# A staging loop in a hybrid attention and mixture-of-experts kernel: four slots in place of two, and its store moved to another queue

## The chip, the cores and the metric

One Trainium2 chip, one launch on its 8 cores. Every core runs the same program on one batch row of 2048 tokens of 1024 numbers, with no exchange between cores. The metric is the device time of the slowest core in microseconds (us).

## The reference

Per batch row (S = 2048 tokens, D = 1024, 16 heads) the layer is a random-feature attention, an FFN block, a channel attention, and the same FFN block again. Only the latent attention `mla` inside the FFN block matters here:

```python
def _L0_ffn_ref(x, ...):
    x = x + mla(rmsnorm(x, w_ln1), W_kvd, W_qd, W_ku, W_qu, W_vu, W_ropeq, W_ropek, W_o)
    x = x + moe(rmsnorm(x, w_ln2), Wg_s, Wu_s, Wd_s, Wg_r, Wu_r, Wd_r, W_router, routing_bias)
    return x

def mla(xn, ...):
    ...
    scores = jnp.where(causal[None, None], scores, jnp.finfo(scores.dtype).min)
    probs = jax.nn.softmax(scores, axis=-1)
    y = jnp.einsum('bhqk,bkhd->bqhd', probs, v).reshape(B, S, H)
    return y @ W_o

x = x + _L0_attn_a_ref(_layernorm(x), ...)
x = x + _L0_ffn_ref(_layernorm(x), ...)
x = x + _L0_attn_b_ref(_layernorm(x), ...)
x = x + _L0_ffn_ref(_layernorm(x), ...)
```

## The kernel before

The kernel is written against the five instruction queues by hand. `Prog` (lines 36 to 94) keeps a list for each engine; each instruction of it is preceded by its semaphore waits, so an engine runs its list strictly in order, and a wait holds up everything behind it on that engine. `p.dma(eng, ...)` puts a DMA in the list of `sync` (SP) or `gpsimd` (POOL); its completion adds 16 to the semaphore given. `p.release(name, sem)` notes when a buffer comes free and `p.use(name)` gives the wait for that. Vector instructions add 1 to `s_dv`, matmuls add 1 to `s_mm`.

`phase_mla` (from line 707) runs twice in the program, once in each FFN block. Its flash loop goes over two halves of 8 heads, 4 blocks of 512 queries (`qb`) and the key blocks below the diagonal. The unnormalized output of a head, 64 rows by 512 queries, and one row of softmax sums leave PSUM through a VectorE cast into `SCF[:, 1536:2048]` (buffer `stg`) and are stored by POOL into `d_yraw`, a DRAM tensor of 1040 rows (1024 of values, 16 of sums) by 2048 tokens, with semaphore `s_yd`. `v_yq[qb]` is the count at which query block `qb` is complete for all heads.

Behind the flash loop stands the loop that the change is about (lines 1071 to 1090), once for each of 16 tiles of 128 tokens, `l` = 0 to 15. Call its steps:

- T, on SP: a DMA transpose of `d_yraw[:, 128 l : 128 l + 128]` into a slot of `SCB`, so that tokens lie on partitions. It waits for `v_yq[l // 4]`, the end of the V projection (`vmm_latdone`), and the slot.
- the scaling, on VectorE: a reciprocal of the 16 sums into `STAT[:, 112:128]`, a drain, and 16 multiplications of 64 columns each in place.
- W, on SP: a plain DMA of the slot to `d_y2` (token-major, DRAM), which waits for the last multiplication.

There are two slots (`ytk0`, `ytk1`), each released by W's landing. As T and W are both in SP's list, the order there is T0, W0, T1, W1, and so on: T of the next tile stands behind W of this one, and so behind this tile's scaling.

Then SP transposes `d_y2` back into `SCA`, 8 DMAs for each half of the tokens (lines 1095 to 1110); every one waits for the one ahead of it. The first of them waits also for `(s_dv, s_dv.v)`, that is for VectorE's last multiplication of tile 15. The matmuls with `W_o` (lines 1111 to 1126) of tokens 0 to 1023 wait for the first 8. In the profile the program's `d_y2` is shown as `d_y`.

The queue of POOL holds, around this, the stores of `d_yraw` before the loop, and behind it the weight loads of the mixture of experts, the first of which waits until the `W_o` matmuls are done.

```python
w = [(s_yd, v_yq[l // 4]), (s_mm, vmm_latdone)]
w = list(w) + p.use(f"ytk{l % 2}")
vt = p.dma("sync", slot, APx(d_yraw, 128 * l, [[S, 1040], [1, 128]]),
           s_tp, wait=w, transpose=True)
```

Of the kernel before, what the change touches and what calls it, by code (L numbers as in the profile page):

```python
# [12 lines left out]
S, D, NT, ND = 2048, 1024, 16, 8  # L13
# [86 lines left out]
def APx(t, off, dims):  # L100
    return bass.AP(t, off, [list(d) for d in dims])


def build_nc(stop_after=None):
# [44 lines left out]
    d_y2 = nc.dram_tensor("d_y2", [S, D], BF16, kind="Internal")  # L149
# [4 lines left out]
    def sbt(name, shape, dt=F32):  # L154
        g = nc.sbuf_tensor(name, list(shape), dt)
        t = g.__enter__()
        ctx.append(g)
        return t
# [13 lines left out]
    SCB = sbt("SCB", [128, 8192], BF16)  # L172
# [22 lines left out]
    p = Prog(nc)  # L195
    s_ld = p.sem("s_ld")
    s_tp = p.sem("s_tp")
    s_st = p.sem("s_st")
    s_gld = p.sem("s_gld")
    s_mm = p.sem("s_mm")  # L200
    s_dv = p.sem("s_dv")
    s_ac = p.sem("s_ac")
    s_pp = [p.sem(f"s_pp{i}") for i in range(4)]
    s_wl = [p.sem(f"s_wl{i}") for i in range(3)]
    s_dbg = p.sem("s_dbg")
    s_rl = [p.sem(f"s_rl{i}") for i in range(4)]
    s_tb = p.sem("s_tb")
    s_sc = p.sem("s_sc")
    s_yd = p.sem("s_yd")

    def mm(out_ap, lhsT, rhs, start, stop, wait=(), tp=None):
        def b(e, out_ap=out_ap, lhsT=lhsT, rhs=rhs, start=start, stop=stop, tp=tp):
            return e.matmul(out_ap, lhsT, rhs, start=start, stop=stop, tile_position=tp)  # L213
        return p.on("tensor", b, wait=wait, inc=s_mm, n=1)

    def v_op(name, *a, wait=(), **kw):
        def b(e, name=name, a=a, kw=kw):
            return getattr(e, name)(*a, **kw)  # L218
        return p.on("vector", b, wait=wait, inc=s_dv, n=1)
# [52 lines left out]
    for c in range(ND):  # L272
        v_op("tensor_scalar_mul", STAT[:, ER * c:ER * c + ER],
             STAT[:, ER * c:ER * c + ER], WLN2[:, c:c + 1],
             wait=([(s_ld, v_preload), (s_ld, v_wrt)] if c == 0 else ()))
# [434 lines left out]
    def phase_mla(v_xnt, v_gain):  # L710
        vmm0 = s_mm.v

        def vcol(l):
# [9 lines left out]
              wait=p.use("wb0"))  # L723
# [5 lines left out]
        for (wb, woff, swl, wv_, dsto) in ((WB1, 4096, s_wl[1], vl_wb1, 0),  # L729
                                           (WB1, 6144, s_wl[1], vl_wb1, 4096)):  # L730
            for ic in range(2):
                for lb in range(4):
# [3 lines left out]
                    for c in range(ND):  # L736
# [5 lines left out]
                           wait=(w0 if c == 0 else ()))  # L742
# [11 lines left out]
        for h2 in range(2):  # L754
            for c2 in range(2):
                hc = 2 * h2 + c2
                kro = 8320 + 4096 * h2 + 2048 * c2
                for lb in range(4):
# [4 lines left out]
                    for c in range(ND):  # L763
# [4 lines left out]
                           wait=(w0 if c == 0 else ()))  # L768
# [15 lines left out]
        vmm_latdone = 0  # L784
        for h2 in range(2):
            v_scpre = s_sc.v
            for pr in range(4):
                gp = 4 * h2 + pr
                for lb in range(4):
# [3 lines left out]
                    for ic in range(2):  # L793
# [4 lines left out]
                           wait=(w0 if ic == 0 else ()))  # L798
# [4 lines left out]
                         wait=[(s_mm, vm)] + ([(s_sc, v_scpre)]  # L803
                                              if pr == 0 and lb == 0 else []))
# [41 lines left out]
            for pr in range(4):  # L846
                gp = 4 * h2 + pr
                for lb in range(4):
# [3 lines left out]
                    for ic in range(2):  # L852
# [6 lines left out]
                           wait=(w0 if ic == 0 else ()))  # L859
# [46 lines left out]
            if h2 == 1:  # L906
                p.release("wb2", s_mm)
                vmm_latdone = s_mm.v
# [8 lines left out]
            for hl in range(8):  # L917
# [3 lines left out]
                if par == 0:  # L921
                    for pj in range(2):
# [7 lines left out]
                              s_sc, wait=w0)  # L930
# [10 lines left out]
                    for kb in range(4):  # L941
# [3 lines left out]
                           wait=p.use(f"ps{bk}") + [(s_dv, v_sqk)])  # L945
# [8 lines left out]
                    for kb in range(4):  # L954
                        p.release(f"ps{kbank[kb]}", s_dv)
                    v_op("tensor_mul", SCF[:, 0:2048], qslab, qslab,
                         wait=[(s_mm, vmm_k)])
                    p.drain("vector")
                    v_sqq = s_dv.v
                    for qb in range(4):  # L960
# [3 lines left out]
                           wait=p.use(f"ps{bk}") + [(s_dv, v_sqq)])  # L964
# [11 lines left out]
                    for qb in range(4):  # L976
# [9 lines left out]
                         wait=[(s_mm, vm_mh)] + p.use("mhcols"))  # L986
# [7 lines left out]
                for qb in range(4):  # L994
# [4 lines left out]
                    for kc in range(nkc):  # L999
# [8 lines left out]
                        if prev is not None:  # L1008
# [5 lines left out]
                               wait=[v_pt, (s_dv, v_vh)] + (w5 if pkc == 0 else []))  # L1014
# [9 lines left out]
                        else:  # L1024
                            if jst > 0:
# [3 lines left out]
                                 wait=[(s_mm, vm), (s_dv, v_mh)] + (wpt if jst == 0 else []))  # L1029
# [3 lines left out]
                                 wait=[(s_ac, va)])  # L1033
# [9 lines left out]
                       wait=[v_pt, (s_dv, v_vh)] + (w5 if pkc == 0 else []))  # L1043
                    p.release(f"pt{pslot}", s_mm)
                    if qb == 3:
# [5 lines left out]
                         wait=[(s_mm, vm_pv)] + wst)  # L1051
                    p.drain("vector")
                    p.release("ps5", s_dv)
                    vd = s_dv.v
# [14 lines left out]

        v_y2h1 = None  # L1070
        for l in range(NT):
            slot = SCB[:, (l % 2) * 1040:(l % 2) * 1040 + 1040]
            w = [(s_yd, v_yq[l // 4]), (s_mm, vmm_latdone)]
            w = list(w) + p.use(f"ytk{l % 2}")
            vt = p.dma("sync", slot, APx(d_yraw, 128 * l, [[S, 1040], [1, 128]]),
                       s_tp, wait=w, transpose=True)
            v_op("reciprocal", STAT[:, 112:128], slot[:, 1024:1040],
                 wait=[(s_tp, vt)])
            p.drain("vector")
            for h_ in range(H):  # L1080
                v_op("tensor_scalar_mul", slot[:, 64 * h_:64 * h_ + 64],
                     slot[:, 64 * h_:64 * h_ + 64], STAT[:, 112 + h_:113 + h_])
            p.drain("vector")
            vd = s_dv.v
            p.dma("sync", APx(d_y2, 128 * l * D, [[D, 128], [1, D]]), slot[:, 0:1024],
                  s_pp[l % 2], wait=[(s_dv, vd)])
            p.release(f"ytk{l % 2}", s_pp[l % 2])
            if l == 7:
                v_y2h1 = (s_pp[0].v, s_pp[1].v)
        v_y2 = (s_pp[0].v, s_pp[1].v)  # L1090
        if stop_after == "mla_trip":
            dump_dbg()
            return True
# [2 lines left out]
        for half in range(2):  # L1096
            for c in range(ND):
                src = APx(d_y2, half * 1024 * D + c * 128, [[D, 1024], [1, 128]])
                w = [(s_tp, s_tp.v)]
                if c == 0 and half == 0:  # L1100
                    w += [(s_pp[0], v_y2h1[0]), (s_pp[1], v_y2h1[1]),
                          (s_mm, vmm_latdone), (s_dv, s_dv.v)]
                elif c == 0:
                    w += [(s_pp[0], v_y2[0]), (s_pp[1], v_y2[1])]
                p.dma("sync",
                      SCA[:, c * S + 1024 * half:c * S + 1024 * half + 1024],
                      src, s_tp, wait=w, transpose=True)
            if half == 0:
                v_y2t_h1 = s_tp.v
# [199 lines left out]
    def phase_ffn(call):  # L1309
# [7 lines left out]
        if phase_mla(v_xnt, v_gain):  # L1317
            return True
# [284 lines left out]
```

How the kernel before makes its waits and increments, by code:

```python
        def f(e, build=build, w=w, inc=inc, n=n):  # L54
            for s, v in w:
                e.wait_ge(s.h, v)
            ins = build(e)
            if inc is not None:
                ins.then_inc(inc.h, n)
# [6 lines left out]
        def f(e, ps=ps):  # L66
            for s, v in ps:
                if v > 0:
                    e.wait_ge(s.h, v)
```

## Time and profile before

| | us |
|---|---|
| median of the 2 runs shown | 7717.26 (7558.05 and 7876.47) |
| profiled execution, device time | 7573.67 |
| its span, slowest core (core 2) | 7571.9 |
| spans of all 8 cores | 7530.7 to 7571.9 |
| busy in that span: TensorE / VectorE / ScalarE / GpSimd | 5157.2 / 2487.9 / 1403.9 / 243.4 |

The span of a core runs from its first instruction to its last. Busy times of engines overlap, and a share of the whole span is a mean over stages with different limits, so the stretch of the loop has to be read by itself. In the rows, PE is TensorE's matmuls, PEld its weight loads, DVE is VectorE, ACT ScalarE, POOL GpSimd, SP SyncE; a "q" behind the name (SPq, DVEq) is the engine's instruction queue. L213, L218, L223, L78 and L79 are the helpers through which matmuls, VectorE and ScalarE operations, DMA transposes and plain DMAs are issued, so instructions are told apart by their tiles. `A<-B` writes A from B. PEclk is the granted TensorE clock as a share of its full 2.4 GHz.

### The profile page before, as it was taken

The page shows a single profiled execution, that of the slowest core. Times are in us where ns is not written, and L with a number is a line of the kernel's source. Part 1 is how long each engine was busy: PE and PEld are TensorE (multiplying, and loading weights), DVE is VectorE, ACT ScalarE, POOL GpSimd, SP SyncE. Part 2 cuts the span into 40 slices and gives each one's busy share as a digit, 9 for nine tenths or more (in the row PEclk, how much of TensorE's full clock was granted, in tenths as well). Part 3 has the DMA queues.
Part 4 walks back from the last instruction along what each step waited for, and adds up shares of the span by engine and source line. Part 5 has one row for each costly group of instructions (what it writes and reads, how often), then busy time and mean ns, then how long its engine had stood idle before and what let it go on. Part 6 is the DMA issues. An engine that isn't in the chain of part 4 may idle for free.

```text
span 7571.9 us, 83246 instructions; the slowest of 8 cores (7530.7 to 7571.9 us)
## 1 busy us (share of the span) xinstructions
PE 5157.2 (68%) x21469; PEld 2065.1 (27%) x21856; DVE 2487.9 (33%) x5348; ACT 1403.9 (19%) x2392; POOL 243.4 (3%) x403
## 2 busy tenths in 40 slices
PE   3556554565662587999996864565652677999995
PEld 1222222111110233444442422111110333444442
DVE  3333335324222413222223455324222423222221
ACT  1221220242441101111111010342441101111110
POOL 0000000000000000000000000000000000000000
PEclk9556566677665798999997976677675788999997
DMA  3001112001002431222224021001002431222223
GB/s 80 4 6 17 17 34 61 9 12 19 13 10 57 102 67 21 36 34 45 34 34 76 3 42 50 10 11 23 10 9 62 96 67 23 34 45 34 34 34 89
DMA packets 280243, 277.60 MB, mean 37 GB/s; under 512 B 181649, under 2 KB 188177, under 8 KB 279826
## 3 DMA queue, kind: packets, MB, share of 16 engines
q0 software_dynamic: 81776, 154.36, 12.3%
q1 hardware_dynamic: 198050, 117.89, 6.1%
q8 instruction: 236, 3.87, 0.2%
q14 instruction: 181, 1.48, 0.1%
HBM read 287.73 MB, written 63.05 MB: 46 GB/s over the span
## 4 chain that ended last, share of the span: by engine, by line
PE 59%; DVE 12%; issue 9%; ACT 8%; DMA 6%; DVEq 2%; SPq 1%; ACTq 1%; another core or an unknown queue 0%; POOL 0%; POOLq 0%
PE PS L213 59%; ACT SCF L223 6%; DVE SCF L218 3%; DVE XNT L218 2%; DVE SCB L218 2%; DVEq L73 2%; DVE SM L218 2%; ACT SCA L223 1%; DMA SCB<-d_yraw 1%; DVE SCA L218 1%; DVE STAT L218 1%; SPq L78 1%; DMA d_lo<-SCB 1%; DMA sp_x<-R 1%; DMA SCA<-d_y 1%
## 5 line engine op out<-in xcount | busy, mean ns | idle before, releaser
L213 PE MATMUL PS<-XNT,WB 128*128 128x512 bf16 x9272 | 2068.6, 383 | 97.1 <-ACT SCA L223 52.7
L213 PE MATMUL PS<-WB,SCA 128*128 128x512 bf16 x4766 | 1091.9, 389 | 357.4 <-DMA SCA<-d_y 267.5
L213 PEld LDWEIGHTS PS<-XNT,WB 128*128 128x128 bf16 x9472 | 933.5, 99 | 1225.6 <-issue 142.3
L223 ACT ACTIVATE SCF<-PS,SM 128x512 bf16<-128x512 f32 (+3 forms) x1280 | 771.2, 622 | 1100.2 <-PE PS L213 1008.2
L213 PE MATMUL PS<-SCF,SCA 128*128 128x512 bf16 x1238 | 595.5, 481 | 400.0 <-DVE SCF L218 195.7
L223 ACT ACTIVATE SCA<-PS 128x512 bf16<-128x512 f32 x768 | 444.7, 595 | 2242.0 <-PE PS L213 1998.9
L218 DVE TENSOR_TENSOR SCA<-SCA,PS 128x512 bf16<-128x512 bf16 x512 | 352.5, 688 | 1438.8 <-PE PS L213 1332.3
L213 PEld LDWEIGHTS PS<-WB,SCA 128*128 128x128 bf16 x4864 | 481.5, 100 | 958.9 <-issue 442.5
L213 PE MATMUL PS<-XNT,SCA 128*128 128x512 bf16 x1270 | 619.5, 501 | 44.5 <-ACT SCF L223 18.9
L218 DVE SCALAR_TENSOR_TENSOR R<-PS,STAT,R 128x512 f32<-128x512 f32 x448 | 315.7, 747 | 515.9 <-PE PS L213 515.9
L213 PE MATMUL PS<-IDENTB,SCF 128*128 128x128 bf16 x768 | 97.2, 305 | 509.3 <-DVE SCF L218 509.3
L218 DVE TENSOR_TENSOR SCF<-SCF,CONSTB 128x128 bf16<-128x128 bf16 x512 | 106.3, 208 | 980.0 <-ACT SCF L223 975.9
L213 PEld LDWEIGHTS PS<-SCF,SCA 128*128 128x128 bf16 x1280 | 128.1, 100 | 884.5 <-issue 861.8
L223 ACT ACT_TABLE_LOAD x16 | 20.5, 1283 | 1430.7 <-PE PS L213 696.4
L213 PE MATMUL PS<-WB,XNT 128*128 128x512 bf16 x997 | 232.3, 385 | 7.5 <-DVE SCA L218 4.5
L218 DVE TENSOR_TENSOR R<-PS,R 128x512 f32<-128x512 f32 x192 | 129.8, 690 | 317.6 <-PE PS L213 317.6
L223 ACT ACTIVATE SCF<-R 128x1024 bf16<-128x1024 f32 x96 | 101.4, 1057 | 636.7 <-PE PS L213 442.3
L213 PEld LDWEIGHTS PS<-IDENTB,SCF 128*128 128x128 bf16 x768 | 73.6, 132 | 533.6 <-issue 533.0
L213 PEld LDWEIGHTS PS<-XNT,SCA 128*128 128x128 bf16 x1280 | 128.1, 100 | 324.9 <-issue 324.9
L213 PE MATMUL PS<-SCB,WB 128*128 128x512 bf16 x252 | 91.9, 485 | 183.0 <-DVE XNT L218 181.9
L79 POOL DMA_DIRECT2D d_yraw<-SCF x256 | 132.3, 521 | 2282.1 <-DVE SCF L218 2247.3
L213 PE MATMUL PS<-SCF,CONSTB 128*128 128x512 bf16 (+1 forms) x158 | 61.2, 522 | 198.6 <-DVE SCF L218 198.6
(121 smaller groups left out, 2667.7 us busy)
## 6 DMA issues: line engine op xcount, KB each, us to landing
WB<-wg_r POOLq DMA_DIRECT2D x28, 1024.0 KB, 13.7
WB<-wu_r POOLq DMA_DIRECT2D x28, 1024.0 KB, 24.0
WB<-wd_r POOLq DMA_DIRECT2D x28, 1024.0 KB, 13.0
sp_x<-R SPq DMA_DIRECT2D x8, 2048.0 KB, 16.7
R<-sp_x POOLq DMA_DIRECT2D x8, 2048.0 KB, 28.3
R<-x SPq DMA_DIRECT2D x4, 2048.0 KB
SCA<-XNT SPq DMA_DIRECT2D x32, 256.0 KB, 2.9
d_yraw<-SCF POOLq DMA_DIRECT2D x128, 64.0 KB, 1.9
```

What stands on the lines that cost most here:

```text
L73: self.q[eng].append(lambda e: e.drain())
L78: return e.dma_start(out=out, in_=in_, transpose=True)
L79: return e.dma_start(out=out, in_=in_)
L213: return e.matmul(out_ap, lhsT, rhs, start=start, stop=stop, tile_position=tp)
L218: return getattr(e, name)(*a, **kw)
L223: return getattr(e, name)(*a, **kw)
```

## The change

The loop gets four slots in place of two (`ytk0` to `ytk3`, 4 x 1040 columns of `SCB`). T signals one of four semaphores `s_pp[l % 4]` in place of the shared `s_tp`. W moves from the `sync` list to the `gpsimd` list and signals `s_rl[l % 4]`, which now releases the slot. The waits of the transposes behind the loop name the four new semaphores in place of two. VectorE's instructions are the same. A semaphore `s_y2` is added and never used.

```diff
         for l in range(NT):
-            slot = SCB[:, (l % 2) * 1040:(l % 2) * 1040 + 1040]
+            slot = SCB[:, (l % 4) * 1040:(l % 4) * 1040 + 1040]
             w = [(s_yd, v_yq[l // 4]), (s_mm, vmm_latdone)]
-            w = list(w) + p.use(f"ytk{l % 2}")
+            w = list(w) + p.use(f"ytk{l % 4}")
             vt = p.dma("sync", slot, APx(d_yraw, 128 * l, [[S, 1040], [1, 128]]),
-                       s_tp, wait=w, transpose=True)
+                       s_pp[l % 4], wait=w, transpose=True)
             v_op("reciprocal", STAT[:, 112:128], slot[:, 1024:1040],
-                 wait=[(s_tp, vt)])
+                 wait=[(s_pp[l % 4], vt)])
             p.drain("vector")
             for h_ in range(H):
                 v_op("tensor_scalar_mul", slot[:, 64 * h_:64 * h_ + 64],
                      slot[:, 64 * h_:64 * h_ + 64], STAT[:, 112 + h_:113 + h_])
             p.drain("vector")
             vd = s_dv.v
-            p.dma("sync", APx(d_y2, 128 * l * D, [[D, 128], [1, D]]), slot[:, 0:1024],
-                  s_pp[l % 2], wait=[(s_dv, vd)])
-            p.release(f"ytk{l % 2}", s_pp[l % 2])
+            p.dma("gpsimd", APx(d_y2, 128 * l * D, [[D, 128], [1, D]]),
+                  slot[:, 0:1024], s_rl[l % 4], wait=[(s_dv, vd)])
+            p.release(f"ytk{l % 4}", s_rl[l % 4])
             if l == 7:
-                v_y2h1 = (s_pp[0].v, s_pp[1].v)
-        v_y2 = (s_pp[0].v, s_pp[1].v)
+                v_y2h1 = [(s_rl[i], s_rl[i].v) for i in range(4)]
+        v_y2 = [(s_rl[i], s_rl[i].v) for i in range(4)]
...
                 if c == 0 and half == 0:
-                    w += [(s_pp[0], v_y2h1[0]), (s_pp[1], v_y2h1[1]),
-                          (s_mm, vmm_latdone), (s_dv, s_dv.v)]
+                    w += v_y2h1 + [(s_mm, vmm_latdone), (s_dv, s_dv.v)]
                 elif c == 0:
-                    w += [(s_pp[0], v_y2[0]), (s_pp[1], v_y2[1])]
+                    w += v_y2
```

## Rows read from the trace of the kernel before

**Rows 1.** Waits of core 2: who waited for whom, total us, times, longest.
```profile
PE PS L213 <- DMA SCA<-d_y: 267.5, 2, 135.1
DVE STAT L218 <- DMA SCB<-d_yraw: 120.4, 30, 4.5
```

**Rows 2.** Busy time by stretch; columns as the first line names them.
```profile
core 2: us, PE busy (x) PEld busy (x) DVE busy (x) ACT busy (x) POOL busy (x), PEclk, DMA share, GB/s
2331.70:2435.60 103.90, 0.00 (x0) 0.00 (x0) 43.03 (x272) 0.00 (x0) 1.02 (x2) 0.50 0.30 77
2463.10:2475.60 12.50, 12.47 (x44) 5.15 (x46) 3.46 (x5) 2.30 (x4) 0.00 (x0) 0.76 0.43 75
2475.70:2486.40 10.70, 10.68 (x49) 4.90 (x50) 4.15 (x6) 3.45 (x6) 0.00 (x0) 1.00 0.43 75
```

**Rows 3.** Chain of work that ended last, first block: start us, us, what.
```profile
2331.73 0.25 DVE STAT L218
2332.08 0.82 DVE SCB L218 x5
2333.05 1.47 DVE SCB L218 x10
2334.60 0.35 SPq L79
2335.11 2.99 DMA SCB<-d_yraw
2338.19 0.25 DVE STAT L218
...
2432.76 0.25 DVE STAT L218
...
2435.61 0.34 SPq L79
2436.25 3.30 DMA SCA<-d_y
```

**Rows 4.** The same chain in the second block, its first and last step.
```profile
5723.66 0.25 DVE STAT L218
...
5830.11 3.42 DMA SCA<-d_y
```

**Rows 5.** SP's instructions in order of time: start us, us, instruction.
```profile
2295.73 1.20 SPq L78 DMA_TRANSPOSE SCB<-d_yraw  x1
2334.60 0.35 SPq L79 DMA_DIRECT2D d_y<-SCB  x1
```

**Rows 6.** VectorE and POOL in order of time; in brackets idle time and releaser.
```profile
2314.68 0.69 DVE L218 CAST SCF<-PS 65x512 bf16<-65x512 f32 x1 [0.80 <-PE PS L213]
2315.94 1.04 POOL L79 DMA_DIRECT2D d_yraw<-SCF  x2 [11.87 <-DVE SCF L218]
2330.89 0.69 DVE L218 CAST SCF<-PS 65x512 bf16<-65x512 f32 x1 [0.80 <-PE PS L213]
2332.08 2.43 DVE L218 TENSOR_SCALAR SCB<-SCB,STAT 128x64 bf16<-128x64 bf16 x16
2333.79 1.02 POOL L79 DMA_DIRECT2D d_yraw<-SCF  x2 [16.80 <-DVE SCB L218]
2338.54 2.43 DVE L218 TENSOR_SCALAR SCB<-SCB,STAT 128x64 bf16<-128x64 bf16 x16
```

**Rows 7.** DMA issues: count, KB each, median us from issue to landing.
```profile
d_yraw<-SCF POOLq DMA_DIRECT2D x128, 64.0 KB, 1.9
d_y<-SCB SPq DMA_DIRECT2D x32, 256.0 KB, 2.1
SCB<-d_yraw SPq DMA_TRANSPOSE x32, 3.3
SCA<-d_ya SPq DMA_TRANSPOSE x8, 5.4
```

**Rows 8.** Transposes of 2048 rows back to back on SP, and who waited.
```profile
1017.03 21.66 SPq L78 DMA_TRANSPOSE SCA<-d_ya  x8
1041.33 3.19 PE L213 MATMUL PS<-WB,SCA 128*128 128x512 bf16 x7 [29.12 <-DMA SCA<-d_ya]
```

**Rows 9.** One SP transpose while weights load through POOL's queue.
```profile
6178.06 13.02 SPq L78 DMA_TRANSPOSE SCB<-d_xn  x1
```

More of the change, by code:

```diff
@@ L209, in build_nc @@
     s_yd = p.sem("s_yd")
+    s_y2 = p.sem("s_y2")
     def mm(out_ap, lhsT, rhs, start, stop, wait=(), tp=None):
```

## The prediction

> **What bounds the kernel now.** I read first the waits, for what TensorE, the busiest engine, waits on longest. It stands still twice, 267.5 us together and up to 135.1 us at a time, until the transposes of `d_y` into `SCA` land [rows 1]. These are the ends of the two `phase_mla` calls. The table by stretch shows what goes on in the first: in the 103.9 us of the loop TensorE and ScalarE do nothing, VectorE is busy for 43.03 us, the 16 DMA engines for 0.30 of the time [rows 2]. So nothing is full there; it is latency. The chain of waits then shows one tile as a ring of single steps [rows 3]: scaling from 2331.73 to 2334.52 (2333.05 + 1.47), W's issue at 2334.60, T's issue at 2335.11, its landing 2.99 later, the next scaling at 2338.19. From 2331.73 to the last reciprocal at 2432.76 it is 15 periods of (2432.76 - 2331.73) / 15 = 6.74 us. Of one period 2.79 us is VectorE, and the other 3.9 us are SP's two issues and T's landing. VectorE's wait for T says the same: 120.4 us in 30 times [rows 1]. From the first reciprocal to the first transpose behind the loop it is 2436.25 - 2331.73 = 104.5 us in the first block, and 5830.11 - 5723.66 = 106.5 us in the second [rows 3, 4].
>
> **What the change does to it.** It removes from SP's list, between T of one tile and T of the next, W and with it the wait for the scaling.
>
> *The first four T.* T0 is issued at 2295.73, long before the flash loop ends [rows 5], since it needs only query block 0. T1 to T3 need the same block and now stand right behind it. At an issue of 1.20 us each and 3.3 us to land [rows 5, 7] they are in place by about 2295.7 + 4 x 1.2 + 3.3 = 2304, some 28 us before VectorE is free at 2331.7. Their cover is the last head's flash work, and they sit in no list that this uses; cost nothing. If they slowed a store of `d_yraw` the cost would be at most their own 4.8 us of issue.
>
> *VectorE's pace.* With data in place a tile takes 2.79 us, plus the gap to the next reciprocal. The nearest row for the gap is the cast that ends at 2330.89 + 0.69 = 2331.58 ahead of the reciprocal at 2331.73 [rows 3, 6]: 0.15 us. So 2.94 us a tile. All 16 take 15 x 2.94 + 2.79 = 46.9 us. Then SP starts the first transpose of `d_y`: it waits for the last multiplication, as before, but no longer issues W15 first; 0.08 us, as W's issue comes 0.08 behind the scaling today. Loop: 47.0 us.
>
> *W on POOL.* Today W is issued 0.08 us after the last multiplication. POOL is slower to start. A store of `d_yraw` starts 0.57 us after its cast when VectorE then rests (2315.94 against 2314.68 + 0.69), but 2.21 us after it when the multiplications follow at once (2333.79 against 2331.58) [rows 6]; I see the second distance on all eight cores. In the new kernel multiplications always follow, so I take 2.2 us, bounds 0.6 and, if it has to wait for a pause of VectorE, no fixed end (a rival below). The row says nothing of a loss on VectorE: the 16 multiplications with POOL's two issues among them take 2.43 us, as do the 16 without [rows 6]. I take 0; the upper bound is that POOL's issue, 1.02 / 2 = 0.51 us, stops VectorE once in each tile, 15 x 0.51 x 2 = 15 us. Landing of 256 KB: 2.1 us from SP; from POOL 64 KB takes 1.9 [rows 7]. I take 2.3. Behind W in POOL's list stand only other Ws and weight loads that wait for the `W_o` matmuls.
>
> *The slots.* A slot goes round in: T 3.3, scaling 2.79, W's start 2.2, its landing 2.3, and some 0.3 for three wake-ups, together 10.9 us for four tiles, 2.7 us a tile. That is just under VectorE's 2.94. With T at 3.8 and W at 2.9 it is 12.0, 3.0 a tile; over 12 tiles this costs 0.7 us a block. I allow 1 us a block.
>
> *The DMA engines.* Eight transposes of 2048 rows, back to back, take from 1017.03 to TensorE's start at 1041.33, 3.0 us each, though each one needs 5.4 to land [rows 7, 8]. So they overlap, and 1040 rows cost between 1.2 (SP's issue) and 1.5 us. The share of 0.30 of 6.74 us [rows 2] is 2.0 us of work for T and W of a tile, which fits in 2.94.
>
> *What is late next.* The 8 transposes of `d_y` up to the first `W_o` matmul are one after the other in both kernels (each waits for the last), so they stay, some 27 us. W8 to W15 are needed only by the second 8. TensorE's clock: it is granted 0.50, its 1.2 GHz level, through the loop; when matmuls return, 12.5 us at 0.76, then 1.00 (2.4 GHz) [rows 2]. A pause of about 75 us in place of 132 still leaves it at the low level when work returns, so this cost of about 2 us stays as it is. Other phases wait for TensorE or VectorE and shift along.
>
> **The sum.** First block 104.5 - 47.0 = 57.5, second 106.5 - 47.0 = 59.5, together 117.0; less 2 for the slots, 115. The profiled execution took 7573.67: 7573.7 - 115 = 7459 us, 1.5% less. The median shown, 7717.26, is the mean of two runs 318 us apart; the profiled one belongs with the lower (7558.05), and my number is for such a run.
>
> **Rivals.**
>
> *POOL starves.* The long start of 2.21 us could mean that POOL gets in only when VectorE pauses. The page "SBUF — State Buffer" of the Trainium skill, section on the "DVE blocks DMA" trap, has it so: a DMA of GpSimd has its descriptors written through ports that VectorE locks in its fast modes, here `tensor_scalar`. By its strict form no W would start during a run of tiles. VectorE would do the four tiles in the slots, 4 x 2.94 = 11.8 us, then run dry; W starts after about 0.6, lands after 2.3, T lands after 3.3, and with wake-ups there are 6.4 us of idleness. With 16 tiles in fours that is three pauses, 19 us a block, gain 115 - 38 = 77, time 7497 us. For it: the delay. Against it: POOL's issue at 2333.79 falls amid the multiplications, which last to 2334.51 [rows 6]; it got in with no pause. Chance 0.10.
>
> *Only the issue is saved.* The page "DMA: Bandwidth & Descriptors" of the Trainium skill, section "Issuing engines are not separate DMA queues", says that DMAs from several engines share the 16 DMA engines, and that spreading them saves only the time to issue. As a mechanism here: T and W do not overlap, the ring stays, and only W's issue and the step to T (2335.11 - 2334.60 = 0.51 us) go [rows 3]: 32 x 0.51 = 16 us, 7557 us. A milder form, T and W one after the other but beside the scaling, is 3.3 + 2.1 = 5.4 us a tile, gain 15 x 1.34 x 2 = 40, 7534 us. Against both: the overlap of eight transposes and the share of 0.30 [rows 2, 8]. Chance 0.05.
>
> *Slower: T jams beside POOL's queue.* One transpose beside POOL's weight loads held SP for 13.02 us [rows 9]. If each T from T4 on, issued among POOL's stores, took that, the loop would be some 7.5 + 12 x 13.0 + 6 = 170 us, 65 more in each block, and the kernel would take about 7703 us. It decides from about 7.6 us for each T, (104.5 - 13.5) / 12. Against: that one stood behind loads of 1 MB each; here POOL has at most a few 256 KB stores under way. Chance 0.03.
>
> **Chances and range.** Every tile at VectorE's pace, as summed: 0.78, and its own range is 7441 (7558 less 117) to 7474 (7459 plus the 15 us of the bound on VectorE). POOL starves 0.10, only the issue 0.05, slower 0.03, something I have not seen 0.04. The range reaches over the second and third: 7435 to 7560. A measurement of this kernel can tell about 2% from no change. That is 151 us, and VectorE's own work in the two loops, 2 x 47 us out of 211, leaves only 117 to gain. So faster by over 2% has only the unseen and the spread between executions (the two shown differ by more): 0.07. Within 2% 0.90. Slower by over 2% needs more than the jam gives: 0.03.
>
> **What would show it.** In the stretch from the last cast to the first transpose of `d_y`: about 47 us with VectorE over 0.9 busy (43 of 47); reciprocals 2.9 us apart; VectorE's 30 waits for T gone or under 10 us in all; T0 to T3 issued together while the flash loop runs; POOL's stores of `d_y` about 2.2 us behind each last multiplication; the two waits of TensorE for `SCA` down from 267.5 to about 150. POOL starving would show as three gaps of 6 us with Ws in bunches of four. Stretched multiplications (2.9 in place of 2.43 for 16) would show that POOL stops VectorE. I am wrong if the gap between reciprocals is over 3.5 us, or if the gain in the loops is given back behind them.

## The result and the profile after

| | before | changed kernel |
|---|---|---|
| median of all timed executions | 7816.48 us (10) | 7616.62 us (11) |
| executions compared | 7555.31, 7558.05, 7561.08 | 7445.55, 7446.25, 7447.18, 7447.81, 7515.21 |
| profiled execution, not in either row above | 7573.67 us | 7445.2 us |
| mean span of its 8 cores | 7552.6 us | 7435.3 us |

The ratio of the means of the second row is 0.987, 95% interval 0.981 to 0.993: faster, by less than 2%. In the executions left out of that row, of either kernel, the cores of a die show a lower granted clock and take up to 6% longer, which is why the medians of the first row lie 258 and 169 us above those of the second. The medians of the second row are 7558 and 7447 us, 111 us apart (the expectations below start from 7446).

The waits of the slowest core, core 5 (who waited for whom: total us, times, longest), answer to [rows 1]:

```profile
PE PS L214 <- DMA SCA<-d_y: 154.8, 2, 78.1
DVE STAT L219 <- DMA SCB<-d_yraw: 4.3, 6, 1.6
```

TensorE's two pauses fell from 267.5 to 154.8 us. Over the eight cores their mean went from 267.4 to 154.0, 113.4 us less, and the mean span by 117.3: the gain of the loops is the gain of the kernel. VectorE's 30 waits for transposes have become 6.

The pauses hold the loop and the eight transposes of `d_y` behind it. On the mean of the eight cores the loop went from 105.4 to 48.3 us in the first block and from 105.8 to 47.9 in the second, 115.0 less together. The eight transposes behind it take 0.8 us longer in each block (27.9 us where it was 27.1, from the first of them to the first `W_o` matmul), which gives 1.6 back.

The busy time of the same core by stretch, as in [rows 2]:

```profile
core 5: us, PE busy (x) PEld busy (x) DVE busy (x) ACT busy (x) POOL busy (x), PEclk, DMA share, GB/s
2326.10:2375.50 49.40, 0.00 (x0) 0.00 (x0) 42.99 (x272) 0.00 (x0) 9.19 (x17) 0.51 0.58 146
2403.20:2415.70 12.50, 12.47 (x46) 5.11 (x47) 3.46 (x5) 2.30 (x4) 0.00 (x0) 0.78 0.40 77
2415.80:2426.50 10.70, 10.70 (x51) 4.88 (x50) 4.15 (x6) 3.45 (x6) 0.00 (x0) 1.00 0.39 80
```

The same 43 us of VectorE's work now fit in 49.4 us instead of 103.9. TensorE comes back as before: its granted clock is 0.78 over the first 12.5 us (0.76 before), then 1.00.

VectorE in order of time, core 5 (start us, us, instruction, idle time before and its releaser), around the places where it kept its pace and where it lost it:

```profile
2326.16 0.25 DVE L219 RECIPROCAL STAT<-SCB 128x16 f32<-128x16 bf16 x1 [0.16 <-issue]
2326.51 2.43 DVE L219 TENSOR_SCALAR SCB<-SCB,STAT 128x64 bf16<-128x64 bf16 x16
2329.10 0.25 DVE L219 RECIPROCAL STAT<-SCB 128x16 f32<-128x16 bf16 x1 [0.16 <-issue]
...
2347.65 0.25 DVE L219 RECIPROCAL STAT<-SCB 128x16 f32<-128x16 bf16 x1 [0.71 <-DMA SCB<-d_yraw]
2347.99 2.43 DVE L219 TENSOR_SCALAR SCB<-SCB,STAT 128x64 bf16<-128x64 bf16 x16
2351.99 0.25 DVE L219 RECIPROCAL STAT<-SCB 128x16 f32<-128x16 bf16 x1 [1.57 <-DMA SCB<-d_yraw]
...
2373.03 2.43 DVE L219 TENSOR_SCALAR SCB<-SCB,STAT 128x64 bf16<-128x64 bf16 x16
```

The period, from one reciprocal to the next, is 2.94 us (2329.10 - 2326.16). In the first block four of the eight cores keep it nearly throughout and need 47.0 to 47.3 us from the first reciprocal to the first transpose of `d_y`; the others take 47.7 to 51.0 (core 5: 49.4). The chain of waits of core 5 shows what the lost time is made of:

```profile
2341.25 6.12 DMA d_y<-SCB
2347.43 4.47 DMA SCB<-d_yraw
2351.99 0.25 DVE STAT L219
```

One store of a tile took 6.1 us to land and the transpose into its slot 4.5 more, so the round trip of that slot was longer than VectorE's time for four tiles.

POOL, core 5, in order of time. The first row is the last pair of `d_yraw` stores, the second and third are the first two stores of tiles:

```profile
2328.22 1.02 POOL L79 DMA_DIRECT2D d_yraw<-SCF  x2 [16.73 <-DVE SCB L219]
2329.51 0.59 POOL L79 DMA_DIRECT2D d_y<-SCB  x1 [0.27 <-DVE STAT L219]
2332.45 0.55 POOL L79 DMA_DIRECT2D d_y<-SCB  x1 [2.35 <-DVE STAT L219]
```

The multiplications of tile 0 end at 2326.51 + 2.43 = 2328.94 and its store starts 0.57 us later, with the next multiplications already running. The table of DMA issues (median us to landing) gives for the changed kernel:

```profile
d_y<-SCB POOLq DMA_DIRECT2D x32, 256.0 KB, 3.0
SCB<-d_yraw SPq DMA_TRANSPOSE x32, 4.2
```

Both take longer to land than in [rows 7]: 3.0 us where it was 2.1, and 4.2 where it was 3.3.

### The profile page after: what moved, and what is told of

It is laid out like the page before. It is cut to its first block, busy times and chain, and to the rows that moved or that the text cites. A ratio compares the mean times of both kernels' runs of the same rounds, so it can differ in the third digit from the quotient of the medians.

```text
span 7442.8 us, 83639 instructions; the slowest of 8 cores (7426.5 to 7442.8 us)
## 1 busy us (share of the span) xinstructions
PE 5184.5 (70%) x21856; PEld 2061.7 (28%) x21856; DVE 2486.3 (33%) x5348; ACT 1404.7 (19%) x2392; POOL 260.8 (4%) x435
## 4 chain that ended last, share of the span: by engine, by line
PE 61%; DVE 12%; issue 9%; ACT 8%; DMA 5%; DVEq 2%; SPq 1%; ACTq 1%; POOL 0%; POOLq 0%
PE PS L214 61%; ACT SCF L224 7%; DVE SCF L219 3%; DVE XNT L219 2%; DVEq L73 2%; DVE SM L219 2%; DVE SCB L219 2%; ACT SCA L224 1%; DVE SCA L219 1%; DVE STAT L219 1%; SPq L78 1%; DMA SCA<-d_y 1%; DMA sp_x<-R 1%; DMA d_xn<-SCF 1%; DMA d_lo<-SCB 1%
## 5 line engine op out<-in xcount | busy, mean ns | idle before, releaser
L214 PE MATMUL PS<-WB,SCA 128*128 128x512 bf16 x4864 | 1090.0, 387 | 240.9 <-DMA SCA<-d_y 154.8
## 6 DMA issues: line engine op xcount, KB each, us to landing
WB<-wd_r POOLq DMA_DIRECT2D x28, 1024.0 KB, 12.5
```

## The experiments

### Slots alone

Four slots, but the store stays in SP's list. The edit is shown against the changed kernel, as all below.

```diff
-            p.dma("gpsimd", APx(d_y2, 128 * l * D, [[D, 128], [1, D]]),
-                  slot[:, 0:1024], s_rl[l % 4], wait=[(s_dv, vd)])
+            p.dma("sync", APx(d_y2, 128 * l * D, [[D, 128], [1, D]]),
+                  slot[:, 0:1024], s_w4[l % 4], wait=[(s_dv, vd)])
```

> Four slots, with the store of each tile left in SP's list between the transposes. My theory: the ring is made by the order in that list, not by the slots, so the transpose of the next tile still stands behind this tile's scaling; period 6.7 us, first reciprocal to first transpose of d_y about 104.5 and 106.5 us in the two blocks, undisturbed time as before, 7555 to 7575 us. Rival, the slots were what was missing: the period falls to 2.9 us and the time to about 7446 us.

Measured: 7550.5 and 7553.8 us, where the kernel before took 7556, 7559 and 7561 beside it (and once 7613). TensorE's and VectorE's waits on core 1:

```profile
PE PS L215 <- DMA SCA<-d_y: 271.4, 2, 137.3
DVE STAT L220 <- DMA SCB<-d_yraw: 124.3, 30, 5.4
```

The loops take 104.6 to 108.4 us on the eight cores. Two more slots bring nothing as long as the next transpose stands behind this tile's store in one list.

### The queue alone

Two slots, the store on POOL's queue.

```diff
-            slot = SCB[:, (l % 4) * 1040:(l % 4) * 1040 + 1040]
+            slot = SCB[:, (l % 2) * 1040:(l % 2) * 1040 + 1040]
```

The slot's name is `ytk{l % 2}` in its wait and its release too.

> Two slots, with the store on POOL's queue. My theory: now the slots bind. A slot goes round in a transpose of 3.6 us, scaling 2.8, start of the store 0.6, its landing about 2.8, and wake-ups of 0.4: 10.2 us for two tiles, 5.1 a tile; 14 tiles at 5.1 and two at 2.9 give about 77 us a block in place of 104.5 and 106.5, so 7558 - 57 = about 7501 us. Rival, the queue alone does it: loops of 47 to 50 us and 7446 us. Rival, the queue does nothing: 7558 us.

Measured: 7491.8 to 7497.4 us in four executions, ratio to before 0.992 (0.989 to 0.994). Loops 71.9 to 75.1 us. VectorE now waits at every second tile only, core 4:

```profile
2326.99 0.25 DVE L219 RECIPROCAL STAT<-SCB 128x16 f32<-128x16 bf16 x1 [0.16 <-issue]
2329.92 0.25 DVE L219 RECIPROCAL STAT<-SCB 128x16 f32<-128x16 bf16 x1 [0.16 <-issue]
2337.04 0.25 DVE L219 RECIPROCAL STAT<-SCB 128x16 f32<-128x16 bf16 x1 [4.34 <-DMA SCB<-d_yraw]
2339.98 0.25 DVE L219 RECIPROCAL STAT<-SCB 128x16 f32<-128x16 bf16 x1 [0.16 <-issue]
```

Two tiles go round in 2337.04 - 2326.99 = 10.05 us, where 10.2 were expected. So the queue brings 63 of the 111 us, and the further slots, worth nothing alone, bring the other 48. The store's landing is, on the same core:

```profile
d_y<-SCB POOLq DMA_DIRECT2D x32, 256.0 KB, 2.3
```

With two slots POOL's stores thus land only 0.2 us later than SP's did, and the transposes as fast as before (3.3 us on every core).

### The store on ScalarE's queue

```diff
-            p.dma("gpsimd", APx(d_y2, 128 * l * D, [[D, 128], [1, D]]),
-                  slot[:, 0:1024], s_rl[l % 4], wait=[(s_dv, vd)])
+            p.dma("scalar", APx(d_y2, 128 * l * D, [[D, 128], [1, D]]),
+                  slot[:, 0:1024], s_w4[l % 4], wait=[(s_dv, vd)])
```

> The changed kernel with the store on ScalarE's queue, idle in this stretch, in place of POOL's. In the changed kernel the store from POOL lands in 3.2 us (median, up to 6.1) where SP's landed in 2.1. If POOL's way of issuing is the cause, the landing falls back to 2.1 to 2.6 us, VectorE waits for no transpose and both loops take 47.0 us; the kernel gains 2 to 4 us on 7446. If it is the transposes that run beside it, the landing stays at about 3 us, transposes stay at 4 to 4.5, and the time stays within 1 us of 7446 but for a start that is 0.5 us earlier.

Measured: 7444.4 and 7447.4 us, no difference from the changed kernel that can be told. The landings moved (core 4):

```profile
d_y<-SCB ACTq DMA_DIRECT2D x32, 256.0 KB, 2.5
SCB<-d_yraw SPq DMA_TRANSPOSE x32, 4.0
```

The store lands in 2.5 us in place of 3.0, the transposes stay slow. All eight cores take 47.0 us for the first loop, and seven of them never wait for a transpose. TensorE's two pauses are 149.6 to 151.7 us, on the mean 3 less than in the changed kernel; in the kernel's time that is within the spread. So of the 0.9 us by which POOL's stores land later than SP's did, 0.5 goes with POOL's queue, but only when four slots keep more transfers under way: with two slots it was 0.2 in all. The rest goes with the transposes that run beside. What in POOL's queue costs the 0.5 us, no run shows.

### Half the scaling, with POOL, with ScalarE, and with seven slots

Three kernels show how close the next limit is behind VectorE. All of them leave out the softmax division of heads 8 to 15, so a tile costs VectorE 1.77 us in place of 2.94. They are compared by the length of the loop and not by their times.

```diff
-            for h_ in range(H):
+            for h_ in range(H // 2):
```

> The changed kernel with the multiplications of only the first 8 of 16 heads; heads 8 to 15 of the latent attention go on without their softmax division, which is the part left out. VectorE's work per tile falls from 2.94 to about 1.77 us. If VectorE were far ahead of all else as the bound, the loops would fall from 49.4 to about 28 us. My theory: the ring of a slot is close behind. A transpose of 4.5 us, scaling 1.6, start of the store 0.6, landing 3.2 and wake-ups 0.3 make 10.2 us for four tiles, 2.55 a tile, so the loop takes 4 x 1.8 + 12 x 2.55, about 38 us, and VectorE waits about 10 us a block for transposes.

> The same half scaling (8 of 16 heads keep their softmax division undone), with the store on ScalarE's queue, where it landed in 2.5 us and started at once. The ring of a slot is then 4.0 + 1.6 + 0.1 + 2.5 + 0.3 = 8.5 us for four tiles, 2.1 a tile, so a loop takes about 4 x 1.8 + 12 x 2.1 = 33 us. If the DMA engines or SP's issue of 1.15 us a transpose were what binds, and not the ring, the store's queue would make no difference and the loop would be as long as with POOL.

> Half the scaling (heads 8 to 15 keep their softmax division undone), the store on ScalarE's queue, and seven slots in place of four. With four slots the loops took 40 us on average whichever queue stored, at a DMA share of 0.89 and 215 GB/s. If the round trip of a slot binds, 8.5 us and more over seven slots is under 1.3 us a tile, VectorE (1.77 us a tile) sets the pace, its waits for transposes vanish and the loops take 16 x 1.77 = 28.5 us. If the DMA engines bind, 9 transposes of 266 KB and 15 stores of 262 KB are still to be moved after the start, 6.3 MB, at 215 GB/s 29.5 us, and with the last landing and the last tile 33 to 35 us, with 4 us or more of waits in each block.

Measured, from the first reciprocal to the first transpose of `d_y`, mean and range of the eight cores in the first block: 41.3 us (39.8 to 43.9) with POOL, 40.1 (37.5 to 41.9) with ScalarE, 29.8 (28.7 to 31.7) with ScalarE and seven slots. The means of the second block are 40.7, 38.0 and 29.3. VectorE's waits for transposes in both blocks are 23.7 to 32.7, 21.0 to 27.7 and 1.0 to 4.5 us. The stretch from 2340 to 2355 on core 4, half scaling with POOL:

```profile
2340.00:2355.00 15.00, 0.00 (x0) 0.00 (x0) 9.65 (x59) 0.00 (x0) 3.43 (x7) 0.50 0.89 216
```

and with seven slots, core 5, 2330 to 2345:

```profile
2330.00:2345.00 15.00, 0.00 (x0) 0.00 (x0) 12.81 (x77) 0.00 (x0) 0.00 (x0) 0.50 1.01 231
```

The first two came out 1.3 and 2.7 us apart where 5 were expected, at a DMA share of 0.89 (the mean busy share of the 16 DMA engines), and that looked like full DMA engines. The third shows that they were not: given more slots VectorE runs on close to its own pace (16 x 1.77 = 28.3 us for 16 tiles; the 28.5 of the expectation is a slip). The averages over the whole loop say it more plainly than the 15 us shown. With four slots and ScalarE's queue 12 transposes of 266 KB and 15 stores of 262 KB, 7.1 MB, took 40.1 us, which is 178 GB/s; with seven 6.3 MB took 29.8 us, 212 GB/s. So with four slots it is the slot's round trip that stands next behind VectorE, as expected, but my price for it was too low (38 expected and 41 measured with POOL, 33 and 40 with ScalarE). The landings are longer than the expectation had them: with ScalarE's queue and four slots the slowest core's transposes in the first loop take 4.9 us in place of 4.0 (median), its stores 3.1 in place of 2.5, so what one link of the ring saves comes back in another.

### VectorE at rest while POOL issues

```diff
-                 wait=[(s_pp[l % 4], vt)])
+                 wait=[(s_pp[l % 4], vt)]
+                 + ([(s_yd, v_yraw)] if l == 0 else []))
```

> The changed kernel, and the first reciprocal waits until the last stores of d_yraw have landed, so VectorE rests while POOL issues them. In all kernels so far POOL starts these stores 2.2 us after their cast, while it starts the stores of tiles 0.57 us after the last multiplication. If VectorE's multiplications cause the 2.2 us, POOL now starts at about 0.57 us and the loop begins 0.6 + 0.5 + 1.9 us after the cast, about 3 us, so some 3 us later in each block (a kernel 5 to 6 us slower). If the 2.2 us are POOL's own (its long rest before), POOL still starts at 2.2 us and the loop begins about 4.6 us after the cast.

Core 5, VectorE and POOL in order of time:

```profile
2325.75 0.69 DVE L219 CAST SCF<-PS 65x512 bf16<-65x512 f32 x1 [0.80 <-PE PS L214]
2328.65 1.02 POOL L79 DMA_DIRECT2D d_yraw<-SCF  x2 [17.05 <-issue]
2330.90 0.25 DVE L219 RECIPROCAL STAT<-SCB 128x16 f32<-128x16 bf16 x1 [4.46 <-DMA d_yraw<-SCF]
```

VectorE is idle from 2326.44 to 2330.90, and POOL still starts 2.21 us after the cast. VectorE is not the cause. It is not POOL's rest either: of the 64 stores that follow a cast in the first block of the changed kernel (core 5), the other 63 start after 0.56 to 0.91 us, with rests of 4 to 281 us before them. The 2.21 us come back in both blocks and on all eight cores of the kernel before, the changed kernel and this one. What is special about the last store stays open. The first reciprocal comes 4.5 us after the cast, as the second case had it, and TensorE's two pauses are 160 to 164 us, about 8 more than in the changed kernel. The kernel was timed once, 7507 us, which is too little to price it.

### The chain behind the loop

The 8 transposes of `d_y` in a half no longer wait for one another.

```diff
-                w = [(s_tp, s_tp.v)]
+                w = [(s_tp, s_tp.v)] if c == 0 else []
...
-                      src, s_tp, wait=w, transpose=True)
+                      src, s_tp if half == 0 else s_y2, wait=w, transpose=True)
```

> The changed kernel, and the 8 transposes of d_y in each half no longer wait for one another; the second half has a semaphore of its own. My theory: the 27.7 us from the first of them to the first W_o matmul are eight latencies of 3.3 us in a row, so they shrink to eight issues of 1.15 us and one landing of 4 to 5 us, 13 to 14 us; gain 14 us a block, 7446 - 28 = 7418 us. Rival, the DMA engines bound them: 8 x 1024 rows at 1.5 us for 1040 rows gives 12 us at least, at a doubled 3.0 us each 24 us, gain 4 us a block, 7438 us.

Measured: 7411.7 and 7414.1 us, ratio to before 0.981 (0.977 to 0.985). On core 1, TensorE's waits, and SP and TensorE in order of time:

```profile
PE PS L214 <- DMA SCA<-d_y: 126.7, 2, 64.1
```

```profile
2378.61 26.37 SPq L78 DMA_TRANSPOSE SCA<-d_y  x16
...
2393.16 7.04 PE L214 MATMUL PS<-WB,SCA 128*128 128x512 bf16 x19 [62.61 <-DMA SCA<-d_y]
```

From the first transpose to the first matmul it is 14.6 us where it was 27.7 (2403.2 - 2375.5). TensorE waits 28 us less in all, as expected; the time fell by 34. The other 6 us lie between the two blocks, in code that is the same: from the first `W_o` matmul of the first block to the first reciprocal of the second the mean of the cores is 3264.6 us in the changed kernel and 3258.9 here. There the cores of the changed kernel alone range from 3259 to 3274, so no cause can be given. Freed of the chain, the 16 transposes take 26.37 / 16 = 1.65 us each to issue, not the 1.15 expected.

### An earlier first half

So far the first transpose of `d_y` waits for VectorE's last multiplication of tile 15, and TensorE with it, although its first matmuls need only tiles 0 to 7. This kernel has seven slots, the store on ScalarE's queue, unchained transposes, those of the first half right behind transpose 14, and eight banks of PSUM (the memory that TensorE writes its sums to) in the `W_o` product in place of four. As several things change at once, it prices them only together. Its core:

```diff
+            if l + NSL < NT:
+                vt[l + NSL] = y_in(l + NSL)
+            if l == 7:
+                v_y2t_h1 = y_half(0, s_tp, [(s, s.v) for s in s_w7]
+                                  + [(s_mm, vmm_fl)])
+        v_y2t = y_half(1, s_y2, [(s, s.v) for s in s_w7])
...
-                bk = 2 * (l % 2) + hf
+                bk = 2 * (l % 4) + hf
```

> Seven slots, the store on ScalarE's queue, the transposes of d_y unchained, those of the first half in SP's list behind transpose 14 so that they start when tile 7's store has landed and not when VectorE has done tile 15, and eight PSUM banks in place of four for the W_o product. From the first reciprocal, tile 7's store lands after 8 x 2.94 + 2.5 = 26 us, the eight transposes take 8 x 1.15 + 4.3 = 13.5, so the W_o matmuls start after about 40 us where the changed kernel needs 49.4 + 27.7 = 77. VectorE is done with tile 15 after 47 us, when the matmuls have filled at most five of the eight banks, so they don't stop. Gain 37 us a block: 7446 - 74 = 7372 us. Rival, the matmuls start early and then wait for VectorE or for the second half, whose transposes land only after 47 + 2.5 + 13.5 = 63 us, against 40 + 28 = 68 for the end of the first half's matmuls: if transposes and stores slow one another by more than 5 us it is given back; the gain is then nearer 50 and the time 7396 us.

Measured: 7385.7, 7387.1, 7397.9 and 7398.1 us; ratio to before 0.974 (0.965 to 0.983). It is the fastest of all: its median, 7392, is 55 us below the changed kernel's 7447. It missed the 7372 expected and came out near the rival's 7396. TensorE's two pauses are 94.3 to 95.7 us on the cores where both show. Core 7, SP and TensorE in order of time:

```profile
2351.33 13.69 SPq L78 DMA_TRANSPOSE SCA<-d_y  x8
2365.23 1.22 SPq L78 DMA_TRANSPOSE SCB<-d_yraw  x1
2375.52 11.83 SPq L78 DMA_TRANSPOSE SCA<-d_y  x8
...
2369.59 58.08 PE L216 MATMUL PS<-WB,SCA 128*128 128x512 bf16 x256 [47.92 <-DMA SCA<-d_y]
```

The matmuls start 46.9 us after the first reciprocal at 2322.70, not 40. The first of the eight transposes comes after 28.6 us where 26 were expected: the median store lands in 3.3 us, not 2.5, and transpose 14, which stands ahead in SP's list, waits for the same store and then takes its own 1.2 us to issue. The eight then need 18.3 us to the first matmul where 13.5 were expected, 13.7 of it for their issue. Most of this is not the loop's doing: at the 1.65 us measured behind the loop, eight issues take 13.2, and the same way took 14.6 us there. In these 18.3 us the DMA share is the highest of the stretches shown (the profile's share can come out over 1):

```profile
2351.30:2369.60 18.30, 0.01 (x1) 0.04 (x2) 14.12 (x90) 0.00 (x0) 0.00 (x0) 0.50 1.15 221
```

Transfers and no longer latencies may hold the work here; no run tests it. Once begun, the matmuls of the first block run for 57 to 58 us without a stop on all eight cores, so neither VectorE nor the second half holds them, and in that the rival was wrong.

## Why the prediction was right or wrong

**The time and the range: wrong for the median.** 7459 us was predicted with a range of 7435 to 7560; the median of 11 executions is 7616.62. The step that failed is the last one of the sum, "my number is for such a run". I had seen in the two times shown that executions of one kernel differ by 318 us, took the lower one as the kernel's time, and gave a range made of mechanisms only: in the range the spread between executions was put at nothing, though it was given a chance of its own. A median falls among the longer executions as soon as they are more than half, and six of the eleven lie between 7617 and 7920. That it was six and not five is chance; with five the median would have been 7515, inside the range. For the executions of the second row the sum is 12 us too high (7447). The start accounts for it: the profiled execution of before, 7573.67, is itself 15 us above the median of its row, 7558, and 7558 - 115 = 7443.

**What bounds it: right.** A ring in SP's list, latency and not throughput. The kernel with only the slots shows that it is the order in the list; the kernel with only the queue, that the slots then bind at once.

**The size, 115 us: right**, 111 measured. In the first block loops of 47 us were predicted and 47.0 to 51.0 came; the pauses of TensorE fell to 154, where about 150 was said. VectorE's waits cost 2.7 us on the mean of the cores, where 2 were allowed, and 1.6 us came back behind the loops, where nothing was expected. The change stayed within 2%, the likeliest class (0.90).

**VectorE's pace, 2.94 us: right** to the hundredth, and POOL's issues among the multiplications cost it nothing (2.43 us for 16, as in [rows 6]).

**POOL's start, 2.2 us: wrong**, it is 0.57. I took the one late store of `d_yraw` for an effect of VectorE, since the profile names VectorE's multiplication as its releaser and the other stores ran with VectorE at rest. With VectorE at rest it is late all the same. The error was to explain a row by what ran beside it. The rival in which POOL starves rested on the same reading and falls with it. The page "SBUF — State Buffer" of the Trainium skill says under the "DVE blocks DMA" trap, in its section "SBUF: two separate sides", that GpSimd cannot write a DMA's descriptors while VectorE runs an operation that takes their shared ports. Taken for the whole run of multiplications, as the rival did, this would bring the stores in bunches of four. The trace does not show that: they start 0.57 us behind each tile, among multiplications of 0.15 us each. A lock that lasts one such multiplication would hardly show, and no run here tests an operation that is longer.

**The landings, 3.3 for T and 2.3 for W: too low**, 4.2 and 3.0. I carried over figures from a kernel in which T and W took turns. By luck these errors and the one on POOL's start cancel in the slot's round trip: 10.9 us predicted, 4.2 + 2.79 + 0.57 + 3.0 + 0.3 = 10.9 with the measured terms. That it is close to VectorE's 11.8 for four tiles was right, and it shows in the 0.4 to 2.4 us by which a core waits at worst.

**Only the issue is saved: wrong rival.** By the page "DMA: Bandwidth & Descriptors" of the Trainium skill, section "Issuing engines are not separate DMA queues", issuing from several engines saves only the time to issue. The trace agrees in that no transfer got shorter by the move (the store lands in 3.0 us where it was 2.1). But a list is also an order of waits, and the move took a wait for VectorE out of the transposes' way: 63 us of the 111 by the move alone.

**Slower, the transposes jam: no.** Their median landing is 4.2 us, and VectorE never waits more than 2.4 us for one.

## What to carry to other kernels

When an engine's queue alternates a load for the next tile with a store that waits for this tile's compute, the ring is as long as load, compute and issue together, and more buffers alone do nothing (7550 and 7554 us with four slots, as with two). Move the store to another queue first, then count slots as round trip over the pace of the slowest stage. Take the terms of that round trip with an allowance, since a landing measured alone (2.1, 3.3 us) gets longer once the transfers overlap (3.0, 4.2). After that, look at what the next phase really needs first: here a chain of waits (28 us of TensorE's pauses, 34 of the time) and half of a loop (together with slots, queue and banks about another 20) lay behind the first repair.

## What the runs showed of the hardware

- A 256 KB store issued by POOL starts 0.57 us after the VectorE instruction it waits for, even amid a dense run of 0.15 us multiplications, and slows them by nothing that the trace shows (2.43 us for 16 either way).
- The same store, beside the same transposes, lands in 3.0 us from POOL's queue and in 2.5 us from ScalarE's. With two slots it lands in 2.3 us from POOL's queue, and alone in 2.1 from SP's.
- Eight transposes of 1024 rows take 27.7 us to the first matmul when each waits for the one ahead, and 14.6 us without these waits, at 1.65 us each to issue.
- A DMA share of 0.89 at 216 GB/s was not the DMA engines' limit; with more transfers under way they moved 231 GB/s at a share of 1.01.
- The last store of `d_yraw` in a block starts 2.21 us after its cast in every kernel of this record that was looked at, with VectorE busy or at rest; no run explains it.
